# Selective scan and FFN: FFN blocks placed sooner, seven residual sums on TensorE and ScalarE, three C products on GpSimd at the end

## What is computed

```python
x = einsum(hidden, in_proj_w)                    # 4 batches, 512 channels, 512 times
x = silu(causal_conv4(x) + conv_b)
dt_low, Bm, Cm = split(x_proj_w @ x)             # 16, 16, 16 rows
dt = softplus(dt_w @ dt_low + dt_b);  A = -exp(A_log)
state = state * exp(dt * A) + (dt * x) * B       # scan over time, 16 states a channel
y = sum_n(state * C) + D * x
y = y * silu(layernorm(x_in))
x1 = x_in + y.T
out = x1 + layernorm(x1) @ sum(factors) / sqrt(8) + bias
```

## Time and profile before

| | us |
|---|---|
| time, median of 3 runs | 506.89 |
| time, lowest and highest | 505.04, 507.24 |
| the profiled execution's own time | 503.0 |
| its span, first to last instruction | 501.2 |
| mean granted TensorE clock | 0.952 |
| VectorE busy, GpSimd busy | 469.0, 453.0 |
| TensorE busy, ScalarE busy | 431.6, 346.5 |

### The profile page before, as it was taken

The page is one execution under the profiler, slowest core; times in us unless marked ns, Lnnn a source line. Parts: engine busy times, 40 slices in busy tenths (PEclk is TensorE's granted clock), DMA queues, the critical chain, the costliest instruction groups (busy, mean ns, idle before and its releaser), DMA issues.

```text
span 501.2 us, 4086 instructions
## 1 busy us (share of the span) xinstructions
PE 431.6 (86%) x1028; PEld 179.7 (36%) x1036; DVE 469.0 (94%) x368; ACT 346.5 (69%) x620; POOL 453.0 (90%) x237
## 2 busy tenths in 40 slices
PE   8749869998798669999898699879988989988797
PEld 4214323433343233434333243424433433343343
DVE  5899999999998999999998999999999977999895
ACT  2797746966579868897679767788788693643332
POOL 4379999989898999999998999999999959999992
PEclk9979989999799989999899989989999997989899
DMA  5799745429971000200981000000593000000002
GB/s 185 250 368 335 185 84 116 88 41 233 329 276 56 0 1 0 63 1 27 332 339 43 1 21 1 21 1 0 166 397 157 1 21 21 32 11 21 1 0 84
DMA packets 17871, 53.96 MB, mean 108 GB/s; under 512 B 2724, under 2 KB 3236, under 8 KB 16824
## 3 DMA queue, kind: packets, MB, share of 16 engines
q1 hardware_dynamic: 16696, 45.31, 25.0%
q0 software_dynamic: 1152, 8.39, 8.3%
HBM read 49.24 MB, written 4.46 MB: 107 GB/s over the span
## 4 chain that ended last, share of the span: by engine, by line
POOL 36%; PE 21%; DVE 19%; issue 17%; ACT 4%; DMA 1%; SPq 0%; POOLq 0%; DVEq 0%; ACTq 0%
POOL h L1104 24%; PE y L509 10%; POOL h L1097 9%; DVE dA L953 9%; DVE h L959 3%; DVE h L953 3%; PE work L486 2%; POOL dtu L1090 2%; PE work L409 2%; ACT dA L774 2%; DVE acc L910 1%; PE work L502 1%; PE work L429 1%; DMA w_in<-w_inT 1%; PE work L436 1%
## 5 line engine op out<-in xcount | busy, mean ns | idle before, releaser
L1104 POOL TENSOR_TENSOR h<-b_rep,dtu 128x1024 f32<-128x1024 f32 x127 | 301.8, 2441 | 12.5 <-DMA b_rep<-bc_scratch 11.2
L509 PE MATMUL y<-h,ident 128*128 128x512 f32 x508 | 248.4, 627 | 37.2 <-DVE h L959 35.0
L774 ACT ACTIVATE dA<-dt,a_neg 128x512 f32<-128x512 f32 x256 | 165.7, 679 | 85.1 <-DVE h L959 74.9
L953 DVE TENSOR_TENSOR_SCAN dA<-dA,h 128x1024 f32<-128x1024 f32 x83 | 189.7, 2285 | 4.8 <-ACT dA L774 4.8
L509 PEld LDWEIGHTS y<-h,ident 128*128 128x128 f32 x508 | 96.3, 198 | 173.9 <-issue 108.6
L1097 POOL TENSOR_TENSOR h<-h,c_rep 128x1024 f32<-128x1024 f32 x45 | 107.1, 2382 | 11.8 <-DVE h L953 11.7
L953 DVE TENSOR_TENSOR_SCAN h<-dA,h 128x1024 f32<-128x1024 f32 x45 | 102.5, 2280 | 4.5 <-ACT dA L774 4.5
L959 DVE TENSOR_TENSOR h<-dA,c_rep 128x1024 f32<-128x1024 f32 x82 | 99.8, 1217 | 1.2
L409 PE MATMUL work<-ctx_sb,w_in 128*128 128x512 f32 x60 | 35.0, 716 | 15.1 <-DVE x L995 14.3
L502 PE MATMUL work<-fsum,xnT 128*128 128x512 f32 x64 | 29.2, 598 | 0.0
L910 DVE SCALAR_TENSOR_TENSOR acc<-work,chan,acc 128x511 f32<-128x511 f32 (+2 forms) x30 | 21.7, 731 | 5.3 <-ACT acc L641 5.0
(11 more groups left out here) (132 smaller groups left out, 415.1 us busy)
## 6 DMA issues: line engine op xcount, KB each, us to landing
b_rep<-bc_scratch SPq DMA_DIRECT2D x32, 512.0 KB, 9.3
c_rep<-bc_scratch SPq DMA_DIRECT2D x32, 512.0 KB, 9.0
fsum<-factors POOLq DMA_DIRECT2D x8, 1024.0 KB, 8.2
x<-x SPq DMA_DIRECT2D x4, 1024.0 KB, 8.5
out<-x SPq DMA_DIRECT2D x16, 256.0 KB, 2.0
ctx_sb<-ctxT SPq DMA_DIRECT2D x3, 512.0 KB, 4.1
ctx_sb<-ctxT SPq DMA_DIRECT2D x2, 256.0 KB, 3.8
w_in<-w_inT SPq DMA_DIRECT2D x1, 384.0 KB, 4.4
```

The costliest lines, as they stand in the source:

```text
L509: mm = pe.matmul(y[:], ident[:], h[:, (s * PAIRS + j) % H_RING, i, :], start=False, stop=(j == sum_order(s)[-1] and i == 1))
L774: act.activation(dA[:, j % 2, i, :], dt[:, k % 2, :], ACT.Exp, scale=a_neg[:, k, 2 * j + i:2 * j + i + 1]).then_inc(exp_done, 1)
L953: dve.tensor_tensor_scan(pair if on_pool(s * PAIRS + j) else decay, decay, pair, 0.0, ALU.mult, ALU.add).then_inc(scanned, 1)
L1104: pool.tensor_tensor(h[:, (s * PAIRS + j) % H_RING], b_rep[:, j], dtu[:, k % 2, :].unsqueeze(1).to_broadcast([P, 2, L]), ALU.mult).then_in ...
```

## The change

- **Residual sum.** In steps 1, 2, 3, 7, 9, 10 and 11 `turn_y` first puts x1's block into `work0` with an identity matmul, then adds the four turned tiles by plain matmuls in place of transposes. VectorE's `add_x1` falls away there; ScalarE copies the sum to `x1` at slot 3 (`x1_evac`). The eight other residual sums stay with VectorE.
- **FFN blocks of batches 0 and 1.** Block 0 keeps its statistics, and its LAYER goes to (5, 3); blocks 1 to 7 have MEAN, VAR, NORM at slots 4, 5, 6, TURN after the seventh sum of the same step, EVAC at slot 0 of the next, and LAYER at its start, a whole step sooner than before.
- **Factor mean.** ScalarE's copy of the mean goes from (4, 7) to (4, 4). The four centre pieces go from (5, 2), (5, 4), (5, 5), (5, 6) to (4, 6), (4, 7), (5, 0), (5, 1), and their scaling from slots 4 to 7 of step 5 to slots 0 to 3.
- **Blocks of batch 2.** All their parts come a few slots sooner.
- **End.** Step 15 has three C products on GpSimd in place of four. Slices of batch 3's layer go from slots 5 and 6 to 3 and 5 of step 14 on TensorE; of block 3's two slices one goes ahead of the last state sum, one behind it.

The diff, of whose tables one or two lines stand:

```diff
@@ -42,14 +42,14 @@
-SCALE_SLOTS = (4, 5, 6, 7)
-CENTRE_SLOTS = (2, 4, 5, 6)
+SCALE_SLOTS = (0, 1, 2, 3)
+CENTRE_SLOTS = ((4, 6), (4, 7), (5, 0), (5, 1))
-RAW_STATS = {8: ((12, 5), (12, 6), (12, 7)), 9: ((13, 0), (13, 1), (13, 1)),
-RAW_LAYER = {8: (13, -1), 9: (13, 2), 10: (13, 6), 11: (14, 1)}
-RAW_FINAL = {8: (13, 2), 9: (13, 5), 10: (14, 0), 11: (14, 4)}
+RAW_STATS = {8: ((12, 3), (12, 4), (12, 4)), 9: ((12, 5), (12, 6), (12, 6)),
+RAW_LAYER = {8: (12, 5), 9: (13, -1), 10: (13, 3), 11: (14, -1)}
+RAW_FINAL = {8: (13, 0), 9: (13, 2), 10: (13, 6), 11: (14, 2)}
...
 EARLY_SUM_ORDER = (1, 0, 2, 3, 5, 4, 6, 7)
 POOL_C = (0, 2, 4)
-LAST_POOL_C = (0, 2, 4, 5)
+LAST_POOL_C = (0, 2, 4)
 SUM_ORDER = (1, 0, 3, 2, 5, 4, 6, 7)
-LAST_SUM_ORDER = (1, 0, 3, 2, 4, 6, 5, 7)
+LAST_SUM_ORDER = (1, 0, 3, 2, 5, 4, 6, 7)
 C_LAG = 3
+TENSOR_RESIDUAL = (0, 1, 2, 6, 8, 9, 10)
 SQ_SCALE = 3.0 ** -0.5
...
         def blocks_at(part, s, at):
 
-            early = {t: ((t + KB, 5), (t + KB, 6), (t + KB, 7), (t + KB + 1, 0), (t + KB + 1, 4),
-                         (t + KB + 2, -1), (t + KB + 2, 2)) for t in range(2 * KB)}
-            early[2 * KB - 1] = early[2 * KB - 1][:LAYER] + ((3 * KB, 5), (3 * KB + 1, 0))
+            early = {t: ((t + KB, 4), (t + KB, 5), (t + KB, 6), (t + KB, 6), (t + KB + 1, 0), (t + KB + 1, -1),
+                         (t + KB + 1, 2)) for t in range(2 * KB)}
+            early[0] = ((KB, 5), (KB, 6), (KB, 7), (KB + 1, 0), (KB + 1, 4), (KB + 1, 3), (KB + 1, 7))
             if part <= NORM:
...
             def turn_y(s):
 
+                b, k = divmod(s, KB)
+                if s in TENSOR_RESIDUAL:
+                    pe.wait_ge(x_landed, (b + 1) * 16)
+                    pe.matmul(work0[:].rearrange("p (t d) -> p t d", t=KB), ident[:], x1_columns(b, k),
+                              start=True, stop=False)
+                    pe.wait_ge(gated, s + 1)
+                    for t in range(KB):
+                        mm = pe.matmul(work0[:, t * P:(t + 1) * P], yg[:, t * P:(t + 1) * P], ident[:], start=False,
+                                       stop=(t == KB - 1))
+                    mm.then_inc(y_turned, 1)
+                    return
                 pe.wait_ge(gated, s + 1)
...
 
             def last_layer(t):
+                if t == 0:
+                    pe.wait_ge(f_scaled, KB)
+                    pe.wait_ge(bias_split, 3)
                 pe.wait_ge(t_xnT, t + 1)
...
                     for t in blocks_at(TURN, s, i):
                         turn_xn(t)
-                    if i in (1, 4) and s < STEPS - 1:
+                    if i in (1 + k % 2, 4) and s < STEPS - 1:
                         for w in w_at(s)[i // 4:i // 4 + 1]:
...
                     for t in [t for t in RAW_LAYER if RAW_LAYER[t] == (s, i)]:
                         raw_layer(t)
-                    if s == STEPS - 2 and i == 5:
+                    if s == STEPS - 2 and i == 3:
                         pe.wait_ge(d_dt, STEPS)
                         z_layer(0, (0, 1))
-                    if s == STEPS - 2 and i == 6:
+                    if s == STEPS - 2 and i == 5:
                         pe.wait_ge(r_final, KB)
                         z_layer(1, (0, 1))
                     if s == STEPS - 1 and i == 1:
                         pe.wait_ge(w_evac, len(W_ORDER))
                         z_layer(2, (0, 1, 2))
-                    if s == STEPS - 1 and i == 2:
+                    if s == STEPS - 1 and i == 3:
                         z_layer(0, (2,))
                         z_layer(1, (2,))
+                    if s == STEPS - 1 and i == 6:
+                        pe.wait_ge(mulc, dve_products(STEPS * PAIRS - 2))
+                        z_layer(3, (0,))
                     if i == 5 and new_batch:
...
             pe.wait_ge(diag_ready, KB)
             for s in range(STEPS):
-                if s == KB + 2:
-                    pe.wait_ge(f_scaled, KB)
-                    pe.wait_ge(bias_split, 3)
                 step(s)
-            pe.wait_ge(mulc, dve_products(STEPS * PAIRS - 2))
-            z_layer(3, (0,))
+            z_layer(3, (1,))
             for half in range(2):
                 turn_y_half(half)
             for t in range(KB):
                 if t == KB - 1:
-                    z_layer(t, (1, 2))
+                    z_layer(t, (2,))
                 pe.wait_ge(z_late, t // 2 + 1)
...
                 act.activation(x1_block(t // KB, t % KB), work1[:], ACT.Copy).then_inc(t_final, 1)
 
+            def x1_evac(s):
+
+                b, k = divmod(s, KB)
+                act.wait_ge(y_turned, s + 1)
+                act.wait_ge(g_done, (b + 1) * KB)
+                act.activation(x1_columns(b, k), work0[:].rearrange("p (t d) -> p t d", t=KB), ACT.Copy
+                               ).then_inc(x1_added, 1)
+
             def decay(s, k, j, i):
...
                         for i in range(KB):
                             nb(g_r, g_mv, i, g_expv, 1, g_nb)
-                    if s == KB and j == 7:
+                    if s == KB and j == 4:
                         act.wait_ge(f_mean, 1)
...
                         act.wait_ge(g_nb, (b + 1) * KB)
                         minus_mean(g_mv, b + 1, k, g_scratch, g_mean)
+                    if j == 3 and s - 1 in TENSOR_RESIDUAL:
+                        x1_evac(s - 1)
                     if j == 3 and k == KB - 2 and b + 1 < BATCH:
                         act.preload_act_table_set("silu_and_others")
                         silu_batch(b + 1)
                         act.preload_act_table_set("natural_log_exp_and_others")
                     if j == 4 - k % 2 and is_g:
                         var_sum(g_mv, b + 1, k, g_scratch, g_mean, s + 1, g_var)
-                    if j in (2 if s == STEPS - 1 else 4 if s > 3 * KB else 5, 7):
+                    if j in (2 if s == STEPS - 1 else 4 if s in (3 * KB, STEPS - 2) else 5, 7):
                         for w in w_at(s)[j // 7:j // 7 + 1]:
                             w_copy(w)
                     for t in blocks_at(EVAC, s, j):
                         if is_g:
-                            act.wait_ge(g_var, s + 1)
+                            act.wait_ge(g_var, s + 1 if j >= KB else s)
                         t_xnT_(t)
...
                     if j == (1 if s < STEPS - 1 else 0) and s > 0:
                         gate_y(s - 1)
-                    if j == (2 + k % 2 if s < STEPS - 1 else 1) and s > 0:
+                    if j == (2 + k % 2 if s < STEPS - 1 else 1) and s > 0 and s - 1 not in TENSOR_RESIDUAL:
                         add_x1(s - 1)
...
                     if j % 4 == 1 and s + j // 4 > 0 and 2 * s + j // 4 < FR:
                         load_factor(2 * s + j // 4)
-                    if s == KB + 1 and j in CENTRE_SLOTS:
-                        centre(CENTRE_SLOTS.index(j))
+                    if (s, j) in CENTRE_SLOTS:
+                        centre(CENTRE_SLOTS.index((s, j)))
                     for t in [t for t in RAW_BIAS if RAW_BIAS[t] == (s, j)]:
```

4 lines of the change are left out of this document (2 added, 2 removed).

## The result

| | before | after |
|---|---|---|
| time, median of 20 runs, us | 504.60 | 509.63 |
| lowest and highest, us | 503.04, 509.17 | 506.74, 512.54 |
| ratio to before, with its 95% interval | | 1.0078 [1.0052, 1.0104] |
| the profiled execution's own time, us | 503.0 | 507.15 |
| its span, us | 501.2 | 505.4 |

The change costs some 4 us by the ratio (the medians are 5.0 apart, the spans 4.2), where the forecast was a gain of 0.9. The median of 509.63 lies at the upper edge of the range of 501 to 510, but that range was built on a median before of 506.89 from three runs, and twenty runs give 504.60.

A forecast was written before the change was run, and what follows sets the result against it. VectorE was taken to bound steps 1 to 12, order step 13 and TensorE the tail. The terms summed to -0.9 us, from a median of 506.89 to 506.0, with a range of 501.0 to 510.0.

The forecast's parts named there:

- What bounds the kernel: Work taken off VectorE pays in steps 1 to 12, order pays in step 13, TensorE sets the tail.
- Residual sums, 0.59 each: Steps 1, 2, 3, 7, 9 and 11: each add taken off VectorE saves 0.59 us, together 3.5.
- Step 10: ScalarE's new copy ahead of the silu tables moves the scan by 0.5; cost taken as 0.3 us.
- The 0.68 of step 11: Slot 1's scan waited 0.68 for decays behind a late projection; TensorE working sooner removes it, -0.7 us.
- The copy of the mean, +6.3: Steps 4 and 5: ScalarE and GpSimd wait for the mean and delay scans, 4.5 + 1.6 + 0.2 us.
- Step 6, +0.1: Statistics at slot 4 instead of 5 cost some 0.1 us each in steps 6 and 8.
- Step 12, +2.1: Block 8's mean ahead of the gate's table load costs 1.3 us; other statistics and a copy add 0.8.
- Step 13, -3.8: Old waits go, a raw final and waits for block 10's layer come: 31.4 us in place of 35.20.
- Step 15, -1.1: Gate's wait goes, -1.5 us; a slice ahead of the last sum, +0.4; the moved C product costs nothing.
- Matmuls in place of transposes: Residual turns: at most 0.9 us extra; if transposes are four times faster, step 10's copy could wait 0.2.
- the third: Slower: ScalarE waits of 0.5 to 0.6 in steps 5 to 11 add 4 us, giving 510.0; chance 0.18.
- The first rival: Faster: step 4 costs 4.5, not 6.3, and block 10's layer runs at full clock; 502.3 us, chance 0.27.

The follow-up runs named there:

- b1: The kernel before with only the early copy of the mean, centre pieces and scaling; median 509.34 us, ratio 1.0074.
- b2: The kernel before with only the seven residual sums moved to TensorE and ScalarE; median 500.84 us, ratio 0.9889.
- b3: The kernel before with both the early copy of the mean and the seven residual sums; two runs, median 513.50 us, ratio 1.0179.
- f1: c1 with three of the four products of block 0's layer left out, so part of the computation is missing; one run, 496.38 us.
- c1: a1 with the statistics of blocks 8, 9 and 10 one slot later; median 497.63 us, ratio 0.9874.
- a1: The changed kernel with the copy of the mean back at (4, 7), centre pieces and scaling later in step 5; median 499.21 us, ratio 0.986.
- c3: a1 with four C products on GpSimd in step 15 and their order of sums as before; median 502.58 us, ratio 0.9932.
- e1: The changed kernel with the copy of the mean one slot later, at (4, 5); one run, 507.34 us.
- e2: The changed kernel with the copy still at (4, 4), but centre pieces and scaling placed as in a1; one run, 508.85 us.
- g2: The same kernel as c1, measured once more; median 499.96 us, ratio 0.9888.

## Why the prediction was wrong

Its own steps, against the traces. The forecast was -0.9 on the span, the trace has +4.2; 5.1 have to be found.

- **What bounds the kernel**: right. Steps 1 to 3 lost time with VectorE's work, waits did the rest.
- **Residual sums, 0.59 each**: the mechanism was right, the size was off. 0.45 each, six times, so the gain was 0.8 smaller. The pitch of 0.59 was read from an add ahead of a scan, and not from what the pitch is without the add. Step 10: the scan of (10, 4) waited 0.82 and started 0.48 later against its step, the 0.5 of the forecast; the step grew by 0.15 by the table, 0.3 forecast, since a wait of 0.26 before (10, 6) went, as it did in b1 without this edit. Against b1's 27.89 it is 0.5. The 0.68 of step 11 went, but it went in b1 too, which has the old sums: it was TensorE's clock in that one trace, and no gain of the change. And after's step 11 is 0.48 longer than b2's: its scan of (11, 1) waits 0.23 for decays behind a turned tile. Step 11 lost 0.75 where 1.3 was forecast (0.59 and 0.7). The smaller sums are 0.8 of the 5.1, and the rest of step 11 0.4.
- **The copy of the mean, +6.3**: the mechanism was right, and alone (b1) it costs 6.33 in waits. The step that failed is to price each edit against the old trace and add up: the term of +6.3 came to +8.3. The residual edit in steps 1 to 3 brought VectorE and ScalarE to slot 3 of step 4 with TensorE ahead of them by more: it waited 2.46 and not 1.70, and did the sum ahead of the mean at half clock, 1.7 slower. The waits are 8.8 in after and 6.3 in b1; that of the one scan is 6.88 in b3, as in after. Steps 4 and 5 grew by 8.3, though the same residual edit had made step 4 shorter by 0.8 (b2). That is 2.0 of the 5.1.
- **Step 6, +0.1**: the term stood for statistics alone, and TensorE's load was left out without a reason. The step grew by 1.8, and with three products of block 0's layer left out it fell to its old length (f1). I wrote that TensorE idles 4.4 of a step, which was read from step 1; in step 6 of after it worked 29.09 of 30.70. That is 1.7.
- **Step 12, +2.1**: right, to 0.01, and in its parts (1.27 more before (12, 4) for 1.3, 0.74 before (12, 5) for 0.8); c1 confirms the place of 1.7 of it.
- **Step 13, -3.8**: -3.66 in the traces, and its wait for block 10's layer was forecast at 2.4 and is 2.28. But the agreement is partly luck: with the old order of the step it is 33.8 to 38.8, with the new one 31.6 to 35.2, and the granted clock of TensorE moves the waits in it. Step 14: -0.65 for -0.7.
- **Step 15, -1.1**: -1.55 in the traces, but the mechanism didn't hold. The gate was to wait no more, -1.5; it still waits 0.91, so that is -0.6. The rest is a wait for `y` near the end that fell from 3.08 to 1.48, and that of 0.61, which is gone. In a1, with the same order there, they are 1.02 and 2.66, and the step is 38.32, only 0.3 below before's. So the agreement is luck. The third C product is nothing in the traces (c3).
- **The start and step 0**: 0.6 longer in the trace of after, with no edit that I could name; the two together took 57.4 to 61.5 in kernels that share their order there. A profiled execution against another can't tell it from chance.
- **The sum**: 0.8 (residual sums), 0.4 (step 11), 2.0 (steps 4 and 5), 1.7 (step 6) and 0.6 (start and step 0) less 0.6 (steps 10 and 15) make 4.9 of the 5.1, and the rest is small. The ends of the forecast were added wrong: by its own terms they are -8.3 and +5.9, not -8.2 and +5.2.
- **Matmuls in place of transposes**: the Trainium skill ("TensorE: Matmul & The Clock Gate", section "Terms") gives a transpose mode that is four times faster for FP32. Here the four transposes of a turned block took 0.60 at full clock and the four matmuls (eight records) 1.05 in after. In step 10 the copy didn't wait for them (ScalarE took it straight behind the decays), so the 0.2 that this factor would have added didn't come, and the trace has nearer two than four.

Of the rivals, the third (ScalarE becomes what the scans wait for in steps 5 to 11) ended on the right side for a wrong reason: steps 7 and 9 show no such wait, step 8 one of 0.90 that before had too, and that of step 10 was in the forecast itself. What the forecast lacked sat mostly in steps 4 to 6. The first rival's opposite happened in step 4: it wasn't less than forecast, it was more. As to the numbers: the median of three runs, 506.89, stood 2.3 above that of twenty, and only for that does 509.63 lie inside the range: put around 504.60 it would be 498.7 to 507.7.

The measured effect is two parts. The early copy and its followers cost 9.1 by a1 against after. All the rest gains 1.4% [1.2, 1.6] by the runs and 3.4 us, 0.7%, by the two traces. By the traces it is the residual sums: steps 1 to 4, 7 and 9 to 11 are 3.6 shorter in a1 than in before (of which 0.8 in step 11 is before's clock), and all other steps together 0.3 longer. The ratio of the residual sums alone, 0.9889 [0.985, 0.9928], can't be told from a1's.

## What to carry to other kernels

An operation that waits for another engine's late result belongs behind everything that someone else is waiting for, on every engine that has a follower of it: here one early copy stopped two engines that both feed the bound one. Moving the copy a slot back on ScalarE alone gave nothing (e1), moving GpSimd's followers back alone gave 2.3 of 9.1 (e2). Prices of single edits don't add where one of them changes how long TensorE stands idle before the step on which another one rests. Nor does taking work off TensorE ahead of a wait have to help: in f1 it came sooner to a wait and was no sooner with the work behind it, and in g2 the same happened without an edit. And compare kernels step by step: most single steps repeated to 0.02 us while whole executions of one kernel were 6 us apart. But a step that hangs on TensorE's clock can be 1.3 to 5 us off in one trace, so such a step wants a second trace.

## What the runs showed of the hardware that I had not expected

- After a wait of 2.46 us TensorE's sum of four records and the product behind it took 6.92 to 7.12 us, in fourteen traces; after one of 1.70 or 1.71 they took 5.42, in two. TensorE had been busy for over 5 us ahead of both waits. The length of the wait alone doesn't decide it. Of all state sums of four records with a wait ahead of them in the sixteen traces, 265 of 267 took at most 2.05 after waits under 1.7, 28 of 37 after waits of 1.7 to 2.4, and 8 of 46 after longer ones.
- The same layer of eight records took 3.70 or 6.62 in two traces of kernels with the same order there (granted clock 1.00 and 0.55). Where VectorE waits for such a layer, this can be a good part of the spread of the whole kernel's time; no run shows how much.
- An operation of VectorE that needs the scan before it starts 2.32 after the scan's start, one that doesn't need it 2.20.
